# A decoder layer on one core: another order of scores and transposes in attention units, and earlier loads at the seams

## The reference

```python
x = x + mamba_bidirectional(layernorm(x))        # forward and backward pass, their projections,
                                                 # a residual on the normed input, layernorm with ln_w, ln_b
x = x + cross_attention(layernorm(x), ctx, mask) # below
x = x + moe_attention(layernorm(x))              # 16 experts' q, k, v of width 64, causal, gated
...
Q, K, V = q @ W_q.T + b_q, ctx @ W_k.T + b_k, ctx @ W_v.T + b_v   # 16 heads of 32
scores = (Q @ K.T) * 32 ** -0.5                  # causal, masked
out = softmax(scores) @ V                        # (batch, head, query, 32)
return out @ W_o.T + b_o
```

## Time and profile before

| | us |
|---|---|
| median of 3 runs | 4629.91 (4629.33 to 4635.51) |
| the profiled execution | 4637.03 |
| its span, first to last instruction | 4635.0 |
| TensorE busy (transposes and products) | 4139.6 (89%) |
| its weight loads | 3072.3 (66%) |
| VectorE | 3183.5 (69%) |
| ScalarE | 1664.6 (36%) |
| GpSimd | 1004.4 (22%) |
| exp, L1665, 512 times | 376.7, idle before 221.8 |
| minimum, L1749, 512 times | 374.7, idle before 55.4 |
| transposes of exps, L1848, 2304 times | 331.4, idle before 25.2 |

### The profile page before, as it was taken

The page is one execution under the profiler, slowest core; times in us unless marked ns, Lnnn a source line. Parts: engine busy times, 40 slices in busy tenths (PEclk is TensorE's granted clock), DMA queues, the critical chain, the costliest instruction groups (busy, mean ns, idle before and its releaser), DMA issues. The chain is left out here.

```text
span 4635.0 us, 72509 instructions
## 1 busy us (share of the span) xinstructions
PE 4139.6 (89%) x26456; PEld 3072.3 (66%) x26456; DVE 3183.5 (69%) x6884; ACT 1664.6 (36%) x3487; POOL 1004.4 (22%) x597
## 2 busy tenths in 40 slices
PE   6999999997898898988858888888898789999998
PEld 5776776764666666656546666566576467777787
DVE  5888888884588887878646646546547476666664
ACT  3333333432333333333226626537437321111111
POOL 1333333242244454444500000000000100000000
PEclk8999999998899999999979999999999899999999
DMA  2111011102011110110143143143142220000000
GB/s 102 35 40 38 26 39 38 40 22 99 17 42 35 45 42 32 49 42 32 36 150 100 42 150 98 61 139 86 62 144 70 78 71 28 28 28 28 28 33 19
DMA packets 144917, 265.89 MB, mean 57 GB/s; under 512 B 25140, under 2 KB 31288, under 8 KB 144568
## 3 DMA queue, kind: packets, MB, share of 16 engines
q1 hardware_dynamic: 144568, 261.27, 17.0%
HBM read 164.58 MB, written 88.08 MB: 55 GB/s over the span
## 5 line engine op out<-in xcount | busy, mean ns | idle before, releaser
L1665 ACT ACTIVATE xa_src<-xa_s,xa_mn 128x896 f32<-128x896 f32 (+7 forms) x512 | 376.7, 738 | 221.8 <-DVE xa_mn L1749 218.4
L1749 DVE TENSOR_REDUCE xa_mn<-xa_s 128x1 f32<-128x896 f32 (+7 forms) x512 | 374.7, 751 | 55.4 <-PE xa_s L1842 49.6
L1848 PE MATMUL xa_gen<-xa_ident,xa_src 128*128 128x128 f32 x2304 | 331.4, 281 | 25.2 <-DVE xa_kq L1774 11.2
L72 PE MATMUL ff_wb<-ff_w_hi,ff_st_hi 128*128 128x512 f32 x768 | 322.5, 420 | 15.7 <-DVE ff_parts L2353 9.9
L1612 POOL TENSOR_TENSOR xa_res<-xa_res,xa_bor 128x512 f32<-128x512 f32 x32 | 40.4, 1267 | 1298.7 <-DMA xa_res<-after_mamba_dram 1298.7
L73 PE MATMUL ff_wb<-ff_w_hi,ff_st_lo 128*128 128x512 f32 x768 | 309.4, 403 | 0.0
L74 PE MATMUL ff_wb<-ff_w_lo,ff_st_hi 128*128 128x512 f32 x768 | 309.3, 403 | 0.0
L1848 PEld LDWEIGHTS xa_gen<-xa_ident,xa_src 128*128 128x128 f32 x2304 | 253.4, 144 | 66.3 <-issue 55.1
L1757 DVE COPY xa_pT<-xa_gen 128x512 f32<-128x512 f32 (+3 forms) x352 | 185.9, 528 | 129.8 <-PE xa_gen L1848 125.8
L1203 PE MATMUL mb_ib<-mb_wc,mb_yT 128*128 128x512 f32 x512 | 268.4, 673 | 1.8 <-DVE mb_y L974 1.0
L2121 POOL TENSOR_TENSOR ff_mixed<-ff_at,ff_rw 128x1024 f32<-128x1024 f32 x32 | 60.9, 1904 | 877.3 <-DVE ff_at L2381 877.3
(11 more groups left out here) (511 smaller groups left out, 11409.4 us busy)
## 6 DMA issues: line engine op xcount, KB each, us to landing
xa_qa<-xa_q_dram SPq DMA_DIRECT2D x384, 64.0 KB, 2.0
xa_q_dram<-xa_kq SPq DMA_DIRECT2D x32, 512.0 KB, 2.8
xa_k_dram<-xa_kq SPq DMA_DIRECT2D x32, 512.0 KB, 2.8
xa_ka<-xa_k_dram SPq DMA_DIRECT2D x192, 64.0 KB, 2.0
xa_st<-xa_k_dram SPq DMA_DIRECT2D x192, 64.0 KB, 2.0
mf_xg<-in_x_dram SPq DMA_DIRECT2D x16, 512.0 KB, 5.4
turned_dram<-mf_xt_hi SPq DMA_DIRECT2D x16, 512.0 KB, 2.6
turned_dram<-mf_xt_lo SPq DMA_DIRECT2D x16, 512.0 KB, 4.0
```

The lines of the kernel that those rows point to most:

```text
L72: nc.tensor.matmul(out, w_hi, x_hi, start=first, stop=False)
L1665: a_.activation(pq[:, hh, 0:w], s1[g, i, hh][:, 0:w], ACT.Exp, scale=-1.0, bias=mn[:, i % 2, hh:hh + 1], accum_out=sums[:, i // QT, i % QT ...
L1749: v_.tensor_reduce(mn[:, i % 2, hh:hh + 1], s1[g, i, hh][:, 0:(i + 1) * P], AX.X, ALU.min).then_inc(mx_ready.sem, 1)
L1848: last = tr(ps[:, n * P:(n + 1) * P], pq[:, hh, j * P:(j + 1) * P], ident[:])
```

## The change

Five edits:

- In an attention step, score 0 comes first, ahead of the scaling and of head 0's turning; score 1 follows head 0's turning and exp 0, and heads 1 and 2 are turned in a row behind it, ahead of exp 1 and head 3.
- x of the next batch is asked for in two steps, ahead of `o` 2 and of `o` 3; `o` 2 and 3 no longer close the body. Statistics, root and normed tiles are done by halves (`ln` 0 and 1): the first half's statistics and root between `o` 4 and `o` 5, its normed tiles and the second's statistics and root between `o` 5 and `o` 6, the second's normed tiles and the mask between `o` 6 and `o` 7. In batch 0 the mask's load goes behind the first weights, and the mask's step behind the normed tiles.
- `kq` 0 and `kq` 8 wait for the low parts of four tiles; `kq` 1 and `kq` 9 for the rest.
- In the backward pass the last tile's residual is loaded into the halves of `xtok[:, 0]`, during the tile before.
- In the experts' stage the first two weights are asked for ahead of the second load of x.

```diff
@@ -498,6 +498,11 @@
...

+        def residual(c):
+
+            spare = xtok[:, N % 2, :]
+            return (spare[:, 0:D], spare[:, D:2 * D]) if c == N - 1 else (partb[:], xres[:])
+
         def ring(c):
@@ -555,9 +560,18 @@
...

-                    wait(sp, out_ready, c - 1)
-                    sp.dma_start(partb[:], part[b, rows, :]).then_inc(res_loaded.sem, 16)
-                    sp.dma_start(xres[:], x_in[b, rows, :]).then_inc(res_loaded.sem, 16)
+                    def load_residual(c):
+                        b, rows = rows_of(c)
+                        for t, src in zip(residual(c), (part, x_in)):
+                            sp.dma_start(t, src[b, rows, :]).then_inc(res_loaded.sem, 16)
+
+                    if c < N - 1:
+                        wait(sp, out_ready, c - 1)
+                        load_residual(c)
+                    if c == N - 2:
+                        wait(sp, base_ready, inner(c))
+                        wait(sp, res_loaded, 2 * c + 1)
+                        load_residual(N - 1)
                 wait(sp, out_ready, c)
@@ -632,13 +646,13 @@
...
                 wait(pool, xn_ready, c)
-                g_.tensor_tensor(h, h, partb[:], ALU.add).then_inc(res_ready.sem, 1)
+                g_.tensor_tensor(h, h, residual(c)[0], ALU.add).then_inc(res_ready.sem, 1)
                 wait(pool, n_ready, c)
...
                 step.after()
-                g_.tensor_tensor(h, h, xres[:], ALU.add).then_inc(out_ready.sem, 1)
+                g_.tensor_tensor(h, h, residual(c)[1], ALU.add).then_inc(out_ready.sem, 1)

@@ -762,7 +776,7 @@
...
                     wait(act, stored[n % 2], n // 2 - 1)
-                    a_.activation(hb[:, n % 2, :], xres[:], ACT.Identity, bias=xm[:, i:i + 1], scale=xr[:, i:i + 1])\
+                    a_.activation(hb[:, n % 2, :], residual(n)[1], ACT.Identity, bias=xm[:, i:i + 1], scale=xr[:, i:i + 1])\
                         .then_inc(xn_ready.sem, 1)
@@ -1362,18 +1376,22 @@
...
         stored = [sig(f"stored{i}", NT // 2, 16) for i in range(2)]
-        dve_step = sig("dve_step", 2 + RSQRT_STEPS)
+        dve_step = sig("dve_step", 2 * (2 + RSQRT_STEPS))
         const_ready, par_loaded, const_dve = sem("const_ready"), sem("par_loaded"), sem("const_dve")
...

+            yield "load_x", 0
+            yield "load_x", 1
+            for half in range(2):
+                for t in range(QT):
+                    yield "stats", half * QT + t
+                yield "ln", half
+                for t in range(QT):
+                    yield "xn", half * QT + t
             yield "mask", 0
-            yield "load_x", 0
-            for t in range(NT):
-                yield "stats", t
-            yield "ln", 0

@@ -1412,16 +1430,16 @@
...

+                yield from one("score", 0)
                 if scale:
...
                 yield from turns(0)
-                yield from turns(1)
-                yield from one("score", 0)
-                yield from turns(2)
                 yield from one("exp", 0)
                 yield from one("score", 1)
+                yield from turns(1)
+                yield from turns(2)
+                yield from one("exp", 1)
                 yield from turns(3)
-                yield from one("exp", 1)
                 yield from one("score", 2)
@@ -1444,22 +1462,20 @@
...
             yield "scale", scale.pop()
-            yield "o", QT - 2
-            yield "o", QT - 1

...
             yield "load_x", 0, 0
+            yield "load_x", 0, 1
             yield "fetch", 0, 0
+            yield "load_mask", 0, 0
             yield "fetch", 0, 1
...
                 if it == 0:
-                    for t in range(NT):
-                        yield "xn", 0, t
                     yield "split", 0, 0
@@ -1467,18 +1483,27 @@
...
                     yield what, it, n
-                ahead = list(head()) if it + 1 < B else []
-                for what, n in ahead[0:2]:
+                if it + 1 == B:
+                    for t in range(QT - 2, NT):
+                        yield "o", it, t
+                    return
+                yield "load_x", it + 1, 0
+                yield "o", it, QT - 2
+                yield "load_x", it + 1, 1
+                yield "o", it, QT - 1
+                yield "load_mask", it + 1, 0
+                yield "o", it, QT
+                ahead = [n for n in head() if n[0] != "load_x"]
+                cut, end = ahead.index(("xn", 0)), ahead.index(("ln", 1)) + 1
+                for what, n in ahead[:cut]:
                     yield what, it + 1, n
-                for t in range(QT, QT + 2):
-                    yield "o", it, t
-                for what, n in ahead[2:]:
+                yield "o", it, QT + 1
+                for what, n in ahead[cut:end]:
                     yield what, it + 1, n
-                for t in range(QT + 2, NT):
-                    if ahead:
-                        for i in range(4 * (t - QT - 2), 4 * (t - QT - 2) + 4):
-                            yield "xn", it + 1, i
-                    yield "o", it, t
+                yield "o", it, QT + 2
+                for what, n in ahead[end:]:
+                    yield what, it + 1, n
+                yield "o", it, QT + 3

@@ -1487,7 +1512,7 @@
...
         gen, s1, acc = [], [], []
-        for what, n in [*body(), *(("o", t) for t in range(QT, NT))]:
+        for what, n in [*body(), *(("o", t) for t in range(QT - 2, NT))]:
             if what == "src":
@@ -1528,10 +1553,9 @@
...

-                def load_x(_):
+                def load_x(i):
                     sp.wait_ge(turn_full.sem, turn_full.at(it, -1))
-                    for i in range(2):
-                        sp.dma_start(src[:, 4 * i:4 * i + 4, :], half(x_in, i)).then_inc(x_loaded[i].sem, 16)
+                    sp.dma_start(src[:, 4 * i:4 * i + 4, :], half(x_in, i)).then_inc(x_loaded[i].sem, 16)

@@ -1588,7 +1612,7 @@
...

-                return {"fetch": fetch, "mask": mask, "load_x": load_x, "load_ctx": load_ctx, "kq": store, "load": load, "scale": move,
+                return {"fetch": fetch, "load_mask": mask, "load_x": load_x, "load_ctx": load_ctx, "kq": store, "load": load, "scale": move,
                      "o": output}
@@ -1717,14 +1741,15 @@
...
                     last = v_.bn_stats(stat[:, t, :], src[:, t, :])
-                    if t == NT - 1:
+                    if t % QT == QT - 1:
                         step(last)

-                def norm_x(_):
-                    for t in range(NT):
+                def norm_x(half):
+                    mine = slice(half * QT, (half + 1) * QT)
+                    for t in range(half * QT, (half + 1) * QT):
                         last = v_.bn_aggr(mv[:, t, :], stat[:, t, :])
                     step(last)
-                    rsqrt(nc, step, xr[:], mv[:, :, 1], tmp[:, 0, :], tmp[:, 1, :], 1.0, EPS)
+                    rsqrt(nc, step, xr[:, mine], mv[:, mine, 1], tmp[:, 0, mine], tmp[:, 1, mine], 1.0, EPS)

@@ -1809,6 +1834,8 @@
...
                             pe.wait_ge(half_ready, w + 1)
+                        pe.wait_ge(slo_ready.sem, slo_ready.at(it, w * NT + QT - 1))
+                    if m % (2 * NHG) == 1:
                         pe.wait_ge(slo_ready.sem, slo_ready.at(it, (w + 1) * NT - 1))
@@ -1980,10 +2007,10 @@
...
             yield "xT", 0
+            yield "weights", 0
+            yield "weights", 1
             yield "load", 1
             yield "logits", 0
-            yield "weights", 0
-            yield "weights", 1
             yield "gate", 0
```

## The result

| | before | after |
|---|---|---|
| median, us | 4635.51 of 5 (4629.33 to 4638.91) | 4577.12 of 5 (4574.69 to 4584.96) |
| ratio of the runs | | 0.988 (95% interval 0.9866 to 0.9893) |
| span of the profiled execution | 4635.0 | 4575.4 |
| last output product of batch 3 | 3673.35 | 3619.71 |
| exp, 512 times: busy, idle before | 376.7, 221.8 | 378.2, 229.7 |

The account below looks back on a forecast made before the run. No engine is full; waits bound the kernel, in wide attention units (score, minimum, exp, freed banks) and at seams. Terms 33 + 5.4 + 5.0 + 6.7 + 7.8 + 5.7 = 63.6 us gave 4566 us, range 4545 to 4600.

Parts of the forecast that it names:

- unit order: Attention units: score 0 first shortens a wide unit from 9.19 to 8.42 us; 33 us in all.
- last tile of the backward pass: End of the backward pass: residual loads issued a tile earlier end the last sum's wait; 5.4 us.
- start of the attention: First batch: statistics start when x's first half lands, not after the mask; 5.0 us, range 2 to 9.
- kq 8's half wait, four times: Projections: kq 8 needs only low part 11 and loses its 1.67 us wait; 6.7 us over four batches.
- batch ends, three: Batch ends: earlier x in halves brings the fifth source transpose and first projection sooner; 2.6 us each, 7.8 us.
- experts' start: Experts' stage: first weights issued at the stage's start remove the first product's 5.75 us wait; 5.7 us.
- the failed step: Batch end: residual 4 there at 2678.8, output 4 added by VectorE at 80.1 to 80.8 instead of 77.1.
- the chain of 5.3 us: Norm of x: statistics and small steps for one half of four tiles, before its normed tiles; 5.3 us.
- Rival C: Batch ends: residuals arrive late, each end loses 2 us instead of gaining 2.6, start gains 2; 4583 us, chance 0.12.
- ring order: Batch ends: DMAs of one issuing engine start in ring order, so the two small loads cannot pass x.
- The clock rule: Batch ends: an idle array falls to half rate; closing TensorE's hole would return up to 1.8 us each, left out of sum.

Follow-up runs that it names:

- units: The kernel before with only the new order inside the attention units; 4604.9 us, ratio 0.9933.
- short_bias: The changed kernel with GpSimd's addition of the output bias on 8 of the 512 columns; 4567.62 us, ratio 0.9851.
- ends: The kernel before with only x asked for sooner, normed by halves, and the new batch-end sequence; 4636.12 us, ratio 1.0.
- kqwait: The kernel before with only the half waits of the projections; 4617.74 us, ratio 0.9959.
- moe: The kernel before with only the experts' first weights asked for and split ahead of the logits; 4627.55 us, ratio 0.9978.
- early: The changed kernel with both halves of the next x asked for ahead of the outputs' residual rows, and statistics dealt out between additions; 4553.69 us, ratio 0.9824.
- early2: The kernel of early with the last output's residual addition and store put behind low part 3 of the next batch's x; 4542.4 us, ratio 0.9791.

## Why the prediction was right, and where it was not

In the traces the mechanism sums to 52 us, and to 55 with the start read from all traces. The prediction had 63.6, and the runs say 56 (50 to 62). Of the 11 us between 4566 and 4577, 5.6 are the kernel before, whose median was 4629.91 on record and is 4635.51 in the result.

| term | predicted | traces |
|---|---|---|
| unit order | 33 | 32 |
| last tile of the backward pass | 5.4 | 4.9 |
| start of the attention | 5.0 | 2.0 in the two traces, 4.9 in all |
| kq 8's half wait, four times | 6.7 | 7.6 |
| batch ends, three | 7.8 | -0.3 |
| experts' start | 5.7 | 5.9 |
| sum | 63.6 | 52, 55 |

- **Unit order: right, its parts in part by luck.** The wide round is 8.39 us (8.42 worked out), score 2 comes at 4.96 (5.00), held by the transposing banks and not by exp, and a middle group of a batch is 1.8 us shorter (1.8). But step by step, from weighing to weighing at full clock, the units of 1024, 896 and 768 keys gained 0.89, 0.92 and 0.41 us (0.77, 0.73 and 0.3 worked out), and the four narrow ones together lost 0.5 (0); the two errors cancel. The last groups with outputs gained 1.4 more in all and not 4.4. The first group of a batch, with projections between its units, gained 3.2 and not 1.8, which I had not worked out. All steps at full clock from a batch's first exp to its last unit, over the traces with either order, give 8.0 us a batch; the last group's eighth step lies in the seam, which doesn't show its gain (102.2 before, 102.1 in units).
- **Backward pass, kq, experts: right**, each within 1 us, each shown by a kernel of its own.
- **Start: right, but not by the two traces.** In the trace of after x's first half is used 9.45 us after its issue and not 7.9. In the eight other kernels that load x this way it landed after 6.4 to 8.3. From the last backward sum to the end of the first exp it is 93.6 us in after, 89.3 to 92.5 in the seven others that also have kq's half waits, 97.6 in before and 98.8 to 102.2 in three more with the old start. The medians differ by 6.8, which is kq 8's 1.9 and 4.9 for the start. I had not looked for the wait of kq's third product behind the second weight split, 0.5 to 1.6 us in after and those seven.
- **Batch ends: the failed step** is "residual 4, which also waits for a store in the same queue, at 2678.8; GpSimd adds (1.26), VectorE adds output 4 at 80.1 to 80.8", and the chain of 5.3 us behind it. I had output 4's addition 14.0 us after the outputs begin; it came after 15.6, 14.5 and 15.0 at the three ends (before 11.0 to 11.2). The store that residual 4 waits for was in my working, but not that it would itself take 5.0 us behind x. From that addition to the fifth source transpose it is 19.9, 19.1 and 19.9 us where I had 18.6, since GpSimd's additions hold VectorE's steps (by short_bias 2.0, 1.2 and 2.0 us). So the fifth source comes 0.6 us later after the outputs' start than before, and not 1.2 sooner. Rival C had this mechanism, but its loss of 2 us a batch did not come: in ends it is 0.6. In the change the half waits make the seam 1.8 us shorter, 5.4 in three; the table counts kqwait's 1.9 for kq 8 in each and leaves -0.3.
- **The clock** isn't needed for the sum, but it moves single traces. Stretches at half clock add up to 464 us in the profiled execution before and 424 after; in the units 54 and 34, and a stretch of 3.4 us inside a unit costs 1.0 to 1.6 us of it. In the kernel before the last two steps of each batch's first group took 10.1 to 10.3 and 9.3 us where an undisturbed group has 8.79 and 7.84. But moe, which has the same instructions there, has this in one batch of four, and the five other kernels with the old unit order have 24 to 34 us at half clock in the units. So the trace of before is a slow one there, and how much of the difference belongs to the change isn't settled.
- Of the Trainium skill's two rules that the prediction weighed, ring order ("DMA: Bandwidth & Descriptors", Queues, rings and completion order) was the one to trust at the batch ends: the residual row asked for 0.7 us behind x's first half landed 0.6 us behind it, and output 3 waits 5.69 us for it in after and 5.75 in ends. The clock rule ("TensorE: Matmul & The Clock Gate", Why this matters for your kernels) paid nothing at the first batch end after, where an idle hole of TensorE of 2.68 us stayed (3.40 us for the first sixteen transposes, 3.65 for the second). At the second and third, with holes of up to 0.8 and of 2.0 us, the first sixteen took 2.2 and 2.0 us at full clock, and the second sixteen, behind holes of 9.3 and 9.9 us, still 3.65. With the holes closed it was 1.91 us for the first sixteen in early, 1.91 and 2.42 in early2.

## What to carry over

Asking for a large transfer sooner helps only if it goes ahead of the whole chain that it would delay: put between small loads of the same queue it only moved the wait (0.6 us lost at a batch end in ends), put ahead of them, with the statistics dealt out, it took 7 us off each seam. At such a seam, list what VectorE has in its queue ahead of the one step that TensorE waits for, and take out what nobody waits for: moving one addition was worth 15 us. And price an order of engines by hand from one timeline: the unit's round came out to 0.03 us, while a neighbouring order that looked as good cost 21 us, 8 of them in units that I had not worked out. Before a term is called wrong by two traces, read the same stretch in all traces that share its code: the start's 2.0 us became 4.9 that way.

## What the runs showed of the hardware

- **Small VectorE steps are held by GpSimd.** Of the small chained steps (some 0.16 us) in the trace of after, 1398 stand free of GpSimd's tensor operations and none lasts over 0.18 us; of 285 that overlap one, 118 last over 0.5 and up to 2.15 us, each ending within 0.03 us of the GpSimd operation. They are 170 us over their usual length in all; 114 of the 118 stand in the two Mamba passes, and how much of the 170 is on the path no run shows. The Trainium skill ("SBUF — State Buffer", SBUF: two separate sides) has VectorE and GpSimd share a port pair that one of them locks for a whole instruction, on VectorE's side when the operation has two SBUF inputs or runs in a mode that uses both ports. Most of the 118 have two inputs; ten have one, and no run shows their mode. short_bias agrees, as the held step went with the long GpSimd operation beside it.
- **The clock differs between executions of the same instructions**: the units stage of moe and of before takes 1247.7 and 1255.6 us, with 27 and 54 us at half clock in the units. A change of under 10 us in this kernel needs many runs and a reading of its seam, not two spans.
